# Two heads' bands as three bf16 products on TensorE, two heads' bands added by VectorE

## The reference, cut to what matters

```python
q, k, v = heads(xn @ Wq.T) / 4, heads(xn @ Wk.T), heads(xn @ Wv.T)   # 4 batches, 16 heads, 1024 x 16
scores = q @ k.T + rel[:, clip(i - j, 0, 128)]                       # a bias by head and distance
attn = softmax(where(i >= j, scores, -inf))
x = x + (attn @ v) @ Wo.T
```

## Time and profile before

| | |
|---|---|
| median of 3 runs | 2453.97 us |
| the profiled execution | 2455.88 us |
| its span, first to last instruction | 2453.8 us |
| busy: PE, PEld | 2067.1 us, 1556.0 us |
| busy: DVE, ACT, POOL | 1482.1 us, 955.9 us, 308.8 us |
| first and last score matmul (L2273) | 1630.0 us, 2352.8 us |

### The profile page before, as it was taken

How to read it: one execution, slowest core, us unless ns; L and a number is a source line. 1 busy time by engine, 2 the same in 40 slices (tenths; PEclk the granted TensorE clock), 3 DMA queues, 4 the chain that set the end, 5 groups by cost and what they waited for, 6 DMA issues and landing times.

```text
span 2453.8 us, 38491 instructions
## 1 busy us (share of the span) xinstructions
PE 2067.1 (84%) x12810; PEld 1556.0 (63%) x12810; DVE 1482.1 (60%) x4378; ACT 955.9 (39%) x1944; POOL 308.8 (13%) x300
## 2 busy tenths in 40 slices
PE   5689999966999975899999836578998998999966
PEld 3578888855878854788888725424554455545445
DVE  7844444446555578444444388677786686687548
ACT  4222232322333343223233234325555555655643
POOL 4420000022000033300000062311001101100000
PEclk8799999987999987999999967769999999999988
DMA  8111010111000022201010130342242242333002
GB/s 270 54 58 30 27 31 27 32 52 41 1 1 1 1 69 79 84 21 32 27 31 27 33 112 15 77 54 60 41 53 53 54 53 47 59 43 39 3 9 69
DMA packets 84043, 114.83 MB, mean 47 GB/s; under 512 B 12216, under 2 KB 73824, under 8 KB 80736
## 3 DMA queue, kind: packets, MB, share of 16 engines
q1 hardware_dynamic: 77424, 94.80, 17.5%
q0 software_dynamic: 6432, 17.57, 2.2%
HBM read 69.17 MB, written 43.17 MB: 46 GB/s over the span
## 4 chain that ended last, share of the span: by engine, by line
PE 61%; DVE 26%; ACT 4%; issue 4%; DMA 2%; POOL 2%; SPq 0%; DVEq 0%; ACTq 0%; POOLq 0%
PE psum L775 10%; PE psum L777 10%; PE psum L776 10%; PE psum L2294 4%; PE psum L126 4%; PE psum L128 4%; PE psum L127 4%; DVE mt L2182 4%; PE psum L2273 3%; PE psum L862 3%; DVE m L2170 3%; DVE m L2179 2%; PE psum L2253 2%; DVE stats L160 2%; PE psum L2277 2%
## 5 line engine op out<-in xcount | busy, mean ns | idle before, releaser
L2133 ACT ACTIVATE pt<-psum 128x512 f32<-128x512 f32 (+3 forms) x768 | 334.0, 492 | 273.0 <-DVE psum L2208 180.2
L740 DVE SCALAR_TENSOR_TENSOR h<-psum,xg,sg 128x128 f32<-128x128 f32 x592 | 166.6, 344 | 415.6 <-PE psum L862 415.6
L556 ACT ACTIVATE sg<-psum 128x512 f32<-128x512 f32 x180 | 107.7, 598 | 544.2 <-PE psum L777 544.2
L775 PE MATMUL psum<-w_hi,xt_hi 128*128 (+1 forms) x720 | 286.2, 398 | 17.9 <-DVE xt_lo L705 17.3
L776 PE MATMUL psum<-w_lo,xt_hi 128*128 (+1 forms) x720 | 284.2, 395 | 0.0
L777 PE MATMUL psum<-w_hi,xt_lo 128*128 (+1 forms) x720 | 283.7, 394 | 0.0
L2253 PE MATMUL psum<-ks,qs 96*128 96x512 bf16 (+3 forms) x768 | 234.8, 346 | 43.0 <-DMA ks<-qk_scr 18.8
L2273 PE MATMUL psum<-qs,ks 99*128 99x512 bf16 (+3 forms) x768 | 238.3, 333 | 24.7 <-ACT pt L2133 19.1
L775 PE MATMUL psum<-w_hi,ht_hi 128*128 (+1 forms) x720 | 217.1, 302 | 0.3
L2277 PE MATMUL psum<-band,ident_r 128*128 128x256 f32 (+1 forms) x864 | 215.0, 337 | 0.0
L2182 DVE CUSTOM_DVE_ANT_0 mt<-psum,band_q 128x256 bf16<-128x256 f32 (+1 forms) x512 | 204.2, 399 | 17.1 <-PE psum L2253 6.9
(11 more groups left out here) (283 smaller groups left out, 4248.6 us busy)
## 6 DMA issues: line engine op xcount, KB each, us to landing
xg<-w_dram SPq DMA_DIRECT2D x54, 256.0 KB, 3.2
qk_scr<-parts SPq DMA_DIRECT2D x32, 384.0 KB, 2.5
qs<-qk_scr SPq DMA_DIRECT2D x96, 128.0 KB, 7.0
ks<-qk_scr SPq DMA_DIRECT2D x96, 128.0 KB, 7.7
xg<-rows_in SPq DMA_DIRECT2D x74, 132.0 KB, 2.1
rows_out<-yb SPq DMA_DIRECT2D x74, 128.0 KB, 1.7
x<-x_dram SPq DMA_DIRECT2D x4, 1024.0 KB, 8.7
out_dram<-x SPq DMA_DIRECT2D x4, 1024.0 KB, 4.5
```

The source lines that it names most:

```text
L556: act.activation(sg[i % 2][:, :, :], up_banks(i)[:, :, 0:F], ACT.Silu).then_inc(*silu.up())
L740: ins = dve.scalar_tensor_tensor(out=h[i % 2][:, e, :], in0=u[:, e, :], scalar=xg[j % XSLOT][:, at:at + 1], in1=sg[i % 2][:, e, :], op0=AL ...
L775: pe.matmul(out, a[0], b[0], start=first, stop=False)
L2133: act.activation(pt[n % NPT][:, 0:q1 - q0], st_bank(n)[:, 0:q1 - q0], ACT.Exp).then_inc(*exped.up())
```

## The change

The head that TensorE gives up goes to VectorE; what TensorE keeps is added in three bf16 parts instead of two fp32r parts. `HP` becomes 2. The order of heads in a cell becomes 3, 0, 2, 1, so that VectorE's heads stand first and third. In the tables, even pairs of heads get three parts (ScalarE rounds, GpSimd subtracts, ScalarE rounds, GpSimd subtracts), odd pairs one fp32 copy and no parts; a pair takes four rounds of the order instead of three.

```diff
@@ -29,7 +29,7 @@
 HEADS, DH, REL = 16, 16, 128
 HG = 4
 NHG = HEADS // HG
-HP = HG - 1
+HP = HG - 2
 MQ = 32
 BLK, FP6_MAX = 32, 7.5
 LN_EPS = 1e-5
@@ -1545,6 +1545,8 @@
                 on_pe()
                 end_of_stage("linear", [name for part in besides for name in part.KEPT])
 
+        BPARTS = 3
+
         class HeadTables:
 
 
@@ -1552,21 +1554,22 @@
                 self.wo = sb(stack, "wo", [P, KD, D])
                 self.qkv = [split(stack, n, [P, KD, D]) for n in ("wq", "wk", "wv")]
                 self.gb = sb(stack, "gamma_beta", [P, 2, KD])
-                self.ident_r = sb(stack, "ident_r", [P, P], F32R)
-                self.band = sb(stack, "band", [P, 2, NHG, HP, 2 * P], F32R)
-                self.band_dve = sb(stack, "band_dve", [P, NHG, 2 * P])
+                self.ident_b = sb(stack, "ident_b", [P, P], BF16)
+                self.band = sb(stack, "band", [P, BPARTS, NHG, HP, 2 * P], BF16)
+                self.band_dve = sb(stack, "band_dve", [P, NHG, HG - HP, 2 * P])
                 self.band_q = sb(stack, "band_q", [P, HEADS, 2 * P], BF16)
                 self.rel_scr = nc.dram_tensor("rel_scr", (HEADS, RL), F32, kind="Internal").ap()
                 self.line0, self.t_hi, self.t_lo = S("line"), S("table_hi"), S("table_lo")
                 self.flipped, self.fulled, self.flip_turned = S("flipped"), S("full"), S("flip_turned")
-                self.part_ok, self.left_ok, self.band_q_ok = S("band_part"), S("band_left"), S("band_q")
+                self.part_ok, self.rest_ok, self.mid_ok, self.left_ok, self.band_q_ok = (S(x) for x in (
+                    "band_part", "band_rest", "band_mid", "band_left", "band_q"))
 
             def allocate(self, stack):
                 self.flip = sb(stack, "flip", [P, P])
                 self.line = sb(stack, "line", [HEADS, RL])
                 self.far = sb(stack, "far", [HEADS, 1])
                 self.stage = [sb(stack, f"table_stage{i}", [P, KD * D]) for i in range(2)]
-                self.full = sb(stack, "band_full", [P, 2, 2 * P])
+                self.full, self.rest = (sb(stack, s, [P, 2, 2 * P]) for s in ("band_full", "band_rest"))
 
             def order(self):
                 yield [("setup", 0)]
@@ -1581,6 +1584,7 @@
                         yield [("flip", hp)]
                     yield [("flip_turn", hp), ("part", (hp, 0))]
                     yield [("part", (hp, 1))]
+                    yield [("part", (hp, 2))]
 
             USES, KEPT = ("flip", "flip_turn"), ()
 
@@ -1593,10 +1597,6 @@
 
             def staged(self, m):
                 return S.dma(f"stage_in{m % 2}")(m // 2 + 1)
-
-            def heads_of(self, hp):
-                g, h0 = divmod(2 * hp, HG)
-                return g, h0, min(2, HP - h0)
 
             def on_sp(self, kind, i):
                 if kind == "setup":
@@ -1633,7 +1633,7 @@
             def on_pool(self, kind, i, ring):
                 line, far = self.line, self.far
                 if kind == "setup":
-                    pool.tensor_copy(self.ident_r[:, :], ident[:, :])
+                    pool.tensor_copy(self.ident_b[:, :], ident[:, :])
                     pool.memset(line[:, :], MASKED).then_inc(*self.line0.up())
                     pool.wait_ge(*self.line0(1))
                     pool.memset(line[:, P + REL:RL], 0.0).then_inc(*self.line0.up())
@@ -1652,13 +1652,19 @@
                     pool.wait_ge(*self.t_hi(i + 1))
                     pool.tensor_tensor(self.qkv[i][1][:, :, :], view, self.qkv[i][0][:, :, :].bitcast(F32),
                                        ALU.subtract).then_inc(*self.t_lo.up())
-                elif kind == "part" and i[1] == 1:
+                elif kind == "part" and i[1] > 0 and i[0] % 2 == 0:
                     hp, part = i
-                    g, h0, n = self.heads_of(hp)
-                    pool.wait_ge(*self.part_ok(hp + 1))
-                    pool.tensor_tensor(self.band[:, 1, g, h0:h0 + n, :], self.full[:, 0:n, :],
-                                       self.band[:, 0, g, h0:h0 + n, :].bitcast(F32),
-                                       ALU.subtract).then_inc(*self.left_ok.up())
+                    g = hp // 2
+                    if part == 1:
+                        if g:
+                            pool.wait_ge(*self.left_ok(g))
+                        pool.wait_ge(*self.part_ok(hp + 1))
+                        pool.tensor_tensor(self.rest[:, :, :], self.full[:, :, :], self.band[:, 0, g, :, :],
+                                           ALU.subtract).then_inc(*self.rest_ok.up())
+                    else:
+                        pool.wait_ge(*self.mid_ok(g + 1))
+                        pool.tensor_tensor(self.band[:, 2, g, :, :], self.rest[:, :, :], self.band[:, 1, g, :, :],
+                                           ALU.subtract).then_inc(*self.left_ok.up())
 
             def on_act(self, kind, i, ring):
                 if kind == "w_split":
@@ -1668,17 +1674,19 @@
                 elif kind == "flip":
                     act.wait_ge(*self.flipped(i + 1))
                     if i:
-                        act.wait_ge(*self.left_ok(i))
+                        act.wait_ge(*(self.rest_ok(i // 2 + 1) if i % 2 else self.part_ok(i)))
                     act.activation(flat(self.full), ring.bank((kind, i)), ACT.Copy).then_inc(*self.fulled.up())
                 elif kind == "part":
                     hp, part = i
-                    g, h0, n = self.heads_of(hp)
+                    g, by_dve = divmod(hp, 2)
                     if part == 0:
                         act.wait_ge(*self.fulled(hp + 1))
-                        if n < 2:
-                            act.activation(self.band_dve[:, g, :], self.full[:, n, :], ACT.Copy)
-                        act.activation(self.band[:, 0, g, h0:h0 + n, :], self.full[:, 0:n, :],
-                                       ACT.Copy).then_inc(*self.part_ok.up())
+                        act.activation(self.band_dve[:, g, :, :] if by_dve else self.band[:, 0, g, :, :],
+                                       self.full[:, :, :], ACT.Copy).then_inc(*self.part_ok.up())
+                    if part == 2 and not by_dve:
+                        act.wait_ge(*self.rest_ok(g + 1))
+                        act.activation(self.band[:, 1, g, :, :], self.rest[:, :, :],
+                                       ACT.Copy).then_inc(*self.mid_ok.up())
                     if part == 1:
                         act.wait_ge(*self.flip_turned(hp + 1))
                         act.activation(flat(self.band_q[:, 2 * hp:2 * hp + 2, :]),
@@ -1911,7 +1919,7 @@
         NCELL = len(CELLS)
         HALF = BANK // P
         FIRST, LAST = [{c: next(j for j, h in cells if h == c) for c in range(CB)} for cells in (CELLS, CELLS[::-1])]
-        HEAD_OF = (HG - 1, *range(HG - 1))
+        HEAD_OF = (HG - 1, 0, HG - 2, 1)
         NU = BATCH * NHG
         LATER = slice(BT, NT)
         QORDER = [x for pair in zip(range(BT - 1, -1, -1), range(BT // 2)) for x in pair]
@@ -2127,7 +2135,7 @@
                             if n >= NPT:
                                 act.wait_ge(*value(n // HG - 2))
                             if near_of[cell] and h >= HP:
-                                act.wait_ge(*biased(u * len(near_cells) + near_cells.index(cell) + 1))
+                                act.wait_ge(*biased((u * len(near_cells) + near_cells.index(cell)) * (HG - HP) + HG - h))
                             else:
                                 act.wait_ge(*score(n + 1))
                             act.activation(pt[n % NPT][:, 0:q1 - q0], st_bank(n)[:, 0:q1 - q0],
@@ -2205,7 +2213,7 @@
                             if near_of[i[1]] and h >= HP:
                                 at = st_bank(n)[:, 0:b1 - q0]
                                 dve.wait_ge(*score(n + 1))
-                                dve.tensor_tensor(at, at, band_dve[:, i[0] % NHG, q0 - j * P:b1 - j * P],
+                                dve.tensor_tensor(at, at, band_dve[:, i[0] % NHG, h - HP, q0 - j * P:b1 - j * P],
                                                   ALU.add).then_inc(*biased.up())
                         elif kind == "y_turn":
                             u, t4 = divmod(i, CB)
@@ -2273,10 +2281,10 @@
                             ins = pe.matmul(bank[:, 0:q1 - q0], ks[r][:, h, j * P:(j + 1) * P], qs[r][:, h, q0:q1],
                                             start=True, stop=not by_pe)
                             if by_pe:
-                                for part in range(2):
-                                    ins = pe.matmul(bank[:, 0:b1 - q0], tables.ident_r[:, :],
+                                for part in range(BPARTS):
+                                    ins = pe.matmul(bank[:, 0:b1 - q0], tables.ident_b[:, :],
                                                     band[:, part, u % NHG, h, q0 - j * P:b1 - j * P],
-                                                    start=False, stop=(part == 1))
```

(1 more changed line is left out.)

## The result

The changed kernel takes 2476.66 us (median of 5 runs, 2473.07 to 2478.14) against 2454.3 beside it; the ratio is 1.0076, interval 1.006 to 1.0091: slower, by 19 us by the ratio. Forecast were 2471 and a range of 2446 to 2490.

The account below looks back on a forecast made before the run. The prediction had TensorE and VectorE hold each other in the heads through two rings of three PSUM banks. Adds 22.1 less relief 6.4 gave 15.7, plus tables 1: 16.7 us slower, 2471 us, range 2446 to 2490.

Parts of the forecast that it names:

- TensorE's relief: Heads: 864 band products stay but get cheaper in bf16, 17.3 us less, 0.37 on the path, 6.4 us gained.
- VectorE's adds: Heads: a second head's adds cost VectorE 42.2 us, 0.52 of it on the path, 22.1 us lost.
- a steady unit: Sign, in heads units with neither projection nor output product: 37.2 us before, 38 to 39 if right.
- L2216's share of the chain: Sign, in the heads: the line of VectorE's add would have near 5% of the chain of waits.
- The last two units: End of the heads, VectorE 31% busy: new add mostly hidden, units not longer and may gain.
- The order: Heads: two waits on `biased` per band cell instead of one, no new stop of its own, 0 us.
- The tables: Table building before the heads: extra copies and passes, pairs moved into batch 0's projection; 1 us, bounds -1 and 7.
- The first score: Sign, start of the heads: scores start within 3 us of 1630.0; many microseconds later would mean tables under-priced.
- A: Rival, heads: TensorE binds, its relief counts in full, adds fill VectorE's idle time; faster, priced at 2445 us; chance 0.20.
- B: Rival, heads and tables: gain and loss meet, no change, 2454 us; chance 0.15.
- C: Rival, heads: VectorE binds outright, all 42.2 us of adds count, TensorE's relief nothing; 2497 us; chance 0.11.
- D: Rival, heads: three bf16 products no faster than two fp32r, relief 0, 2477 us; chance 0.54 together with the main case.

Follow-up runs that it names:

- bf16_two_parts: The kernel before with TensorE's two band parts and the identity in bf16 instead of fp32r, VectorE's work unchanged: 2450.4 us, ratio 0.9978.
- idle_add: bf16_two_parts plus, at the third step of each band cell, a VectorE add of the same width on a buffer nobody waits for: 2470.5 us, ratio 1.0062.
- first_second: The changed kernel with VectorE's heads first and second in a cell's order, not first and third: 2475.0 us, ratio 1.008.
- tensor_all: The kernel before with TensorE adding all four heads' bands (first part fp32r, second bf16) and VectorE none: 2450.1 us, ratio 0.9977.
- all_bf16: bf16_two_parts with all four heads' bands on TensorE and none on VectorE: 2439.0 us, ratio 0.9933.
- two_fp32r: The changed kernel with two fp32r parts instead of three bf16 parts for TensorE's two heads: 2469.6 us, ratio 1.0063.
- no_add: bf16_two_parts with VectorE's adds and ScalarE's wait for them taken out, so head 3 lacks its band: 2424.6 us, ratio 0.988.

## Why the prediction was right, step by step

TensorE's relief. Priced at 17.3 us, 0.37 of it on the path, 6.4. The traces give 22 (the 128-column step is 0.056, where I had read 0.07 off a pair of other products) and 0.27: 6.0 by bf16_two_parts. A price a fifth too low and a share a third too high cancelled, and the clock helped: without the 1.3 us of unit 5 the relief is 4.7 us and the share 0.21. That this term came out near 6.4 is luck. In order of time, a 128-column score and its three products in the change:

```profile
2221.84 0.23 PE L2281 MATMUL psum<-qs,ks 99*128 99x128 bf16 x1 [0.29 <-ACT pt L2141]
2221.90 0.33 PE L2285 MATMUL psum<-band,ident_b 128*128 128x128 bf16 x3
2222.07 0.38 PE L2261 MATMUL psum<-ks,qs 96*128 96x512 bf16 x1
```

Four products within 0.23 us, where three took 0.29. A bf16 load is shown with 98 ns against 194 for fp32r, 128 columns both, and the step fell with it. The Trainium skill (TensorE: Matmul & The Clock Gate, section "LDWEIGHTS") has the time go by columns alone; the measurement decides against it here. The section "Weight-path perf modes", which the prediction named for the same rule, says more than it took from it: its table has a fast load for weights of 128 columns in types other than fp32, at about twice the speed. The 98 against 194 ns agree with that.

VectorE's adds. 42.2 us and 0.52 of it, 22.1. Measured 22.5, a share of 0.53, with order and tables in it. Less the relief of 4.7 that makes the 18 of the heads at an even clock. Two signs came as named: a steady unit at 38.4 us, and VectorE's waits for scores down from 71.1 to 67.2 us. L2216's share of the chain is 4.0% where I said near 5. A 256-column add still has its neighbour 0.34 us behind:

```profile
2197.05 0.43 DVE L2216 TENSOR_TENSOR psum<-psum,band_dve 128x256 f32<-128x256 f32 x1
2197.39 0.28 DVE L2187 TENSOR_REDUCE m<-psum 128x1 f32<-128x128 f32 x1
```

The mechanism, that it costs by its place in VectorE's queue, is shown by idle_add.

The last two units. I expected the add hidden there for the most part, and perhaps a gain. They are 0.9 us longer, and 1.6 longer than in bf16_two_parts (62.8), so the third-place add is not hidden, although VectorE idles. The idle add costs 0.3 there: this is latency, not load.

The order. Priced at 0; first_second, another order, takes the same time. The old order with two adds was not run.

The tables. Priced at 1, bounds -1 and 7. The first score came 7.5 us late, outside the 3 that I named as the sign. Half of that, 3.6, arose ahead of the stage in which the tables are built (it starts at 1407.5, before at 1403.8), and the other 3.7 is inside the scatter of the experiments. Nothing shows the step right either.

The rivals. A (TensorE binds) falls: its relief is worth 0.2 to 0.27 and not 1. B falls with the interval. C (every add on the path) falls: 0.53. D falls: three bf16 products a head are faster than two fp32r ones at 128 columns and no slower overall than I said. Moving a head onto the busier engine by the profile, TensorE with 92% against 71%, is what made the kernel faster in tensor_all and all_bf16. The Trainium skill's rule to relieve the engine of the highest occupancy (Perfetto Trace Analysis, "Identifying the Most-Contended Engine") would have sent it the other way if matmul time is taken for TensorE's occupancy, against which the page itself warns. By the share of weight loads, one of two measures that it names in place of that, TensorE has 355.0 of 713.6 us, 50%, and VectorE with its 71% is the fuller engine; the runs agree with that reading.

What the shares could not give is the other kernels. A share of the chain holds near the kernel that it is read from: with shares taken from it I was 11 us off on tensor_all and 6 on all_bf16, which take VectorE's part away altogether.

## What to carry to other kernels

Price a shift of work between two engines that hold each other through small rings by each one's share of the chain against its own step times (start to start), not by busy percentages; a matmul's shown duration flatters TensorE's. Use such a share for a small move only: here TensorE's was 0.55 to 0.9 with none of the four heads on VectorE and 0.2 to 0.27 with one. Ahead of reading a difference of a few us between two single executions, look at the granted clock of each stretch: here it hid 2.5 us and more of gain in two_fp32r and made a fifth of the gain in bf16_two_parts. And what a queue must do costs even when nobody waits for its result, because the next thing in that queue is waited for.

## What the runs showed that I had not expected

Bf16 parts are worth having for themselves: for 128 columns a product of the identity by a bf16 band costs 0.056 us from start to start against 0.11 for fp32r, and one weight load 98 ns against 194, so two bf16 parts on all four heads (105 us of TensorE) cost about what two fp32r parts cost on three (101), though their band is coarser. And VectorE's adds weighed more when taken away (0.63 for the first head's) than when added (0.53 for the second's), where one would expect the engine nearer its limit to charge more. Of the 3.9 us between the two, 3.2 lie in the last two units: 58.0 us in no_add, 62.8 in bf16_two_parts, 64.4 in the change. There VectorE idles and ScalarE's wait counts, which no_add takes out as well. In the other fourteen units the two weigh nearly the same, 21.6 and 20.9 us.
